# Attention over 2304 positions: one query tile's upper and lower value sums formed by one 129-column matmul, the lower one added afterwards on VectorE

## The reference, cut to what matters

```
xn   = groupnorm(x)
q, k, v = Wq xn, Wk xn, Wv xn              # per head: 64 channels x 2304 positions
attn = softmax over keys m of (q_n . k_m)  # no scaling by the root of 64
out  = sum over m of attn[n, m] v_m
y    = x + gamma * out + Wsc xn
```

## Time and profile before

| | |
|---|---|
| median of three runs | 3135.88 us |
| profiled execution, its own time | 3136.14 us |
| its span in the profile | 3134.4 us |
| PE busy | 3085.4 us (98%) |
| weight loads (PEld) | 2183.6 us (70%) |
| POOL busy | 2789.6 us (89%) |
| DVE busy, ACT busy | 2271.4 us (72%), 2244.6 us (72%) |
| mean granted TensorE clock | 0.997 |

### The profile page before, as it was taken

How to read it: one execution, slowest core, us unless ns; L and a number is a source line. 1 busy time by engine, 2 the same in 40 slices (tenths; PEclk the granted TensorE clock), 3 DMA queues, 4 the chain that set the end, 5 groups by cost and what they waited for, 6 DMA issues and landing times.

```text
span 3134.4 us, 119616 instructions
## 1 busy us (share of the span) xinstructions
PE 3085.4 (98%) x52307; PEld 2183.6 (70%) x52307; DVE 2271.4 (72%) x3623; ACT 2244.6 (72%) x4020; POOL 2789.6 (89%) x2040
## 2 busy tenths in 40 slices
PE   6999999999999999999999999999999999999998
PEld 4676777767767677776766767777776777777766
DVE  7677777777777777777777777777777777777774
ACT  5666787777676677777767677778776767667675
POOL 1788999999888899999888889999988989889899
PEclk9999999999999999999999999999999999999999
DMA  3111111110111111120112111111101010101011
GB/s 130 30 41 37 32 45 24 45 34 23 36 40 50 29 36 43 25 54 25 24 30 52 47 26 43 35 34 45 24 23 26 20 29 20 29 20 29 20 29 30
DMA packets 168968, 110.78 MB, mean 35 GB/s; under 512 B 120320, under 2 KB 166400, under 8 KB 168448
## 3 DMA queue, kind: packets, MB, share of 16 engines
q1 hardware_dynamic: 168448, 103.13, 12.5%
HBM read 56.10 MB, written 18.87 MB: 24 GB/s over the span
## 4 chain that ended last, share of the span: by engine, by line
PE 88%; POOL 5%; DVE 2%; ACT 1%; issue 1%; POOLq 0%; ACTq 0%; DVEq 0%
PE SL L440 24%; PE PJ L379 19%; PE MX L412 11%; PE OB L461 10%; PE OB L458 9%; PE OB L460 9%; PE PJ L376 6%; POOL PLO L940 5%; PE SL L435 1%; DVE mx L740 0%; DVE stat L896 0%; DVE xr L731 0%; DVE DF L690 0%; ACT QK L540 0%; DVE mx L743 0%
## 5 line engine op out<-in xcount | busy, mean ns | idle before, releaser
L940 POOL TENSOR_TENSOR PLO<-PE 128x768 f16<-128x768 f32 x1728 | 2550.6, 1499 | 278.4 <-ACT PE L554 267.0
L554 ACT ACTIVATE PE<-SL 128x768 f32<-128x768 f32 x1728 | 1307.4, 810 | 26.8 <-PE SL L440 26.6
L458 PE MATMUL OB<-V,PE 128*128 128x65 f16 x10368 | 1049.2, 193 | 7.2 <-POOL PLO L940 6.1
L460 PE MATMUL OB<-V,PE 128*128 128x64 f16 x10368 | 1049.3, 193 | 0.0
L461 PE MATMUL OB<-V,PLO 128*128 128x65 f16 x10368 | 1049.0, 196 | 0.0
L458 PEld LDWEIGHTS OB<-V,PE 128*128 128x128 bf16 x10368 | 965.4, 99 | 58.5 <-POOL PLO L940 12.2
L440 PE MATMUL SL<-QK 64*128 64x384 f16 x10368 | 1001.0, 323 | 0.1
L460 PEld LDWEIGHTS OB<-V,PE 128*128 128x128 bf16 x10368 | 962.9, 97 | 42.9
L562 ACT ACTIVATE MXC<-MX 128x384 f32<-128x384 f32 x864 | 423.5, 490 | 760.5 <-PE MX L412 760.5
L461 PEld LDWEIGHTS OB<-V,PLO 128*128 128x128 f16 x10368 | 963.8, 98 | 0.0
L743 DVE TENSOR_REDUCE mx<-MX 128x2 f32<-128x768 f32 x864 | 828.7, 959 | 82.7 <-PE MX L412 38.4
(11 more groups left out here) (104 smaller groups left out, 1238.1 us busy)
## 6 DMA issues: line engine op xcount, KB each, us to landing
gx<-x SPq DMA_DIRECT2D x36, 768.0 KB, 4.7
xr<-x SPq DMA_DIRECT2D x96, 192.0 KB, 2.4
out<-xr SPq DMA_DIRECT2D x96, 192.0 KB, 1.9
X<-x SPq DMA_DIRECT2D x6, 768.0 KB, 8.6
CR<-c SPq DMA_TRANSPOSE x96, 2.3
back<-half SPq DMA_TRANSPOSE x95, 2.8
QK<-wk SPq DMA_DIRECT2D x1, 1024.0 KB, 12.7
QK<-wv SPq DMA_DIRECT2D x1, 1024.0 KB, 13.4
```

The costliest lines, as they stand in the source:

```text
L458: pe.matmul(acc, upper, v[:, D:V1], start=k == 0 and h == 0 and i == 0, stop=False, skip_group_check=True)
L460: pe.matmul(acc[:, 0:D], upper, v[:, 0:D], start=False, stop=False, skip_group_check=True)
L554: act.activation(PE32[:, s % PB, :].rearrange("p (h n) -> p h n", h=2), SL[s % 2][:, :, 0:CH], ACT.Exp, scale=1.0 / SS).then_inc(s_exp, 1)
L940: nc.gpsimd.tensor_tensor(PLO[:, s % PB, :], PE32[:, s % PB, :], PE32[:, s % PB, :].bitcast(BF16)[:, 1:4 * CH:2], ALU.subtract).then_inc(s ...
```

## The change

In each step, the first query tile of the first head (h = 0, i = 0) no longer gets L458 and L460 but one matmul over all 129 columns of V, lower values, upper values and ones. It needs a stationary load less. The sum with the lower values now has 64 columns of its own in OB (0 to 63), and the six tiles of 66 columns start at column D = 64. After `evacuate` VectorE adds these 64 columns to the tile's part of Oe (`add_lower`, placed between `top_other` and the second `top` of m = 1, and ahead of `invert` at the end). A new semaphore `s_ol` tells that it is done; the first `weigh` of a chunk and the divisions wait for it.

```
-                    pe.wait_ge(s_oe, n)
+                    pe.wait_ge(s_ol, n)
...
-            acc = OB[:, (h * QT + i) * OW:(h * QT + i) * OW + AW]
+            acc = OB[:, D + (h * QT + i) * OW:D + (h * QT + i) * OW + AW]
...
-            pe.matmul(acc, upper, v[:, D:V1], start=k == 0 and h == 0 and i == 0, stop=False, ...)
-            pe.matmul(acc[:, 0:D], upper, v[:, 0:D], start=False, stop=False, ...)
+            if h == 0 and i == 0:
+                pe.matmul(OB[:, 0:V1], upper, v, start=k == 0, stop=False, ...)
+            else:
+                pe.matmul(acc, upper, v[:, D:V1], start=False, stop=False, ...)
+                pe.matmul(acc[:, 0:D], upper, v[:, 0:D], start=False, stop=False, ...)
...
     evacuate (ACT):
-        act.activation(Oe[:, :, :, :], OB[:, 0:2 * QT * OW] ...
+        act.activation(Oe[:, :, :, :], OB[:, D:D + 2 * QT * OW] ...
     divide (ACT, h == 0) and divide (DVE, last chunk):
+        wait_ge(s_ol, n + 1)
...
+    def add_lower(n):
+        dve.wait_ge(s_oe, n + 1)
+        nc.vector.tensor_tensor(Oe[:, 0, 0, 0:D], OB[:, 0:D], Oe[:, 0, 0, 0:D], ALU.add).then_inc(s_ol, 1)
...
     VectorE's loop, after top_other(U) and before top(U + 1):
+        if m == 1 and n:
+            add_lower(n - 1)
     VectorE's end:
+    add_lower(CHUNKS - 1)
     invert(CHUNKS - 1)
```

More of the change, by code:

```diff
@@ L212, in build @@
         s_oe = sem("s_oe")
+        s_ol = sem("s_ol")
         s_rc = sem("s_rc")
@@ L454, in weigh @@
                         p0 = h * CH + i * P
-                        acc = OB[:, (h * QT + i) * OW:(h * QT + i) * OW + AW]
+                        acc = OB[:, D + (h * QT + i) * OW:D + (h * QT + i) * OW + AW]
                         upper = PE32[:, s % PB, p0:p0 + P].bitcast(BF16)[:, 1:2 * P:2]
                         v = V[:, g % 2, k, h * V1:(h + 1) * V1]
-                        pe.matmul(acc, upper, v[:, D:V1], start=k == 0 and h == 0 and i == 0, stop=False,
-                                  skip_group_check=True)
-                        pe.matmul(acc[:, 0:D], upper, v[:, 0:D], start=False, stop=False, skip_group_check=True)
+                        if h == 0 and i == 0:
+                            pe.matmul(OB[:, 0:V1], upper, v, start=k == 0, stop=False, skip_group_check=True)
+                        else:
+                            pe.matmul(acc, upper, v[:, D:V1], start=False, stop=False, skip_group_check=True)
+                            pe.matmul(acc[:, 0:D], upper, v[:, 0:D], start=False, stop=False,
+                                      skip_group_check=True)
                         last = pe.matmul(acc, PLO[:, s % PB, p0:p0 + P], v[:, D:V1], start=False,
@@ L567, in evacuate @@
                     act.wait_ge(s_wt, n)
-                act.activation(Oe[:, :, :, :], OB[:, 0:2 * QT * OW].rearrange(
+                act.activation(Oe[:, :, :, :], OB[:, D:D + 2 * QT * OW].rearrange(
                     "p (h i x) -> p h i x", h=2, x=OW)[:, :, :, 0:AW], ACT.Copy).then_inc(s_oe, 1)
@@ L574, in divide @@
                     act.wait_ge(s_rc, n + 1)
+                    act.wait_ge(s_ol, n + 1)
                     act.wait_ge(s_al, n)
@@ L794, in divide @@
                 dve.wait_ge(s_rc, n + 1)
+                dve.wait_ge(s_ol, n + 1)
                 dve.wait_ge(s_al, n)
```

## The result

Over 20 runs of each the changed kernel took 3130.62 us against 3135.89 us; the ratio is 0.9983, with a 95% interval of 0.9977 to 0.9989. That is 5.27 us less, a gain that is clear of its interval and smaller than the 0.2% that the prediction had set as its mark. The profiled execution took 3130.39 us with a span of 3128.6 us.

What follows compares the result with a forecast made beforehand. TensorE (PE) was taken to bound the kernel until POOL's splits take over in chunk 90. 3136.14 - 5.7 (merged matmul) + 0.2 (tail) = 3130.6 us, or 3130.4 by the runs' median; 8 in 10 range 3122.5 to 3136.

Steps and rivals of the forecast that it cites:

- The bound and the 1618 steps: PE bounds until POOL's splits take over in chunk 90; only the 1618 `weigh` steps before that can gain.
- The merged matmul: First tile of each `weigh` step: one fixed matmul cost saved, 3.5 ns per step, 5.7 us; bounds 3.2 and 12.3 us.
- The signs: Expected in the trace: first tile about 88 ns instead of 92, other tiles unchanged, POOL taking the chain about 6 us earlier.
- The weight loads don't show in any of them.: PE's matmuls of three widths cost their columns plus a fixed 3 to 3.7 ns; loads of some 100 ns stay hidden.
- The addition: VectorE after `evacuate`: 0.24 us (0.18 to 0.56), ready 0.2 us before PE wants it, costing PE nothing.
- the wait binds: Rival, chance 0.09 with other costs: PE waits for `s_ol` at first `weigh` of 89 chunks, 18 us lost, 3148 us.
- VectorE idle for some 0.9 us: Sign on VectorE before L740: the addition's 0.24 us delay comes out of an idle time of 1.08 us.
- The tail: After the last matmul: addition ahead of the reciprocal adds 0.24 us (0.18 to 0.56); merging saves nothing at the lower clock.
- Only inside the tile: Rival, chance 0.18: in `weigh` only gaps inside the tile shrink, 2.0 ns per step, 3.2 us less, 3132.9 us.
- rate of short matmuls: Rival, chance 0.24: short matmuls' rate limits `weigh`; merging gains 5 to 7.6 ns per step, 8 to 12.3 us less.
- No cheaper: Rival, chance 0.06: the 129-column matmul costs as much as the two it replaces; only the tail counts, 3136.1 us.

Runs made afterwards that it cites:

- e9: Kernel before with a different form of `weigh` in each of a block's six chunks, one having a 16-column second matmul; 3123.61 us (before 3135.51).
- e1: Changed kernel without VectorE's addition and its semaphore, matmuls as changed; 3130.67 us, ratio 0.9986 to the kernel before.
- e2: Kernel before plus the 64-column addition into a spare tile with `s_ol` and PE's wait, matmuls as before; 3136.14 us, ratio 1.0002.
- e10: Changed kernel with a further 384-column addition ahead of the real one, so `s_ol` comes later, traced; 3136.03 us in one execution.
- e4: Changed kernel with all six tiles of a step given the 129-column matmul; 3112.0 us, ratio 0.9931 to the kernel before.
- e11: Changed kernel with the sums ordered so both operands change as rarely as they can; 3123.14 us, ratio 0.9959 to the kernel before.
- e12: The changed kernel as it is, run again on the chip of the rarest-change order; 3130.81 us, ratio 0.9984 to the kernel before.

## Why the prediction was right, step by step

- **The bound and the 1618 steps.** Right. The gain stops at POOL's takeover in chunk 90, and POOL's stage kept its length: 166.9 us against 166.8.
- **The merged matmul.** 3.5 ns per step were taken, between 2.0 and 7.6; 3.27 were measured. The bookkeeping was right (one matmul less, the same columns), the one fixed cost at all widths was not. The 56.7 ns read from the L376 rows are a mean in which the first of 18 starts is followed by 66.3 ns; the others are 55.8 ns apart, 2.5 ns over the columns (over 171 such groups). L458 and L460, where they aren't late, take 29.2 ns, about 2 ns over theirs, and the late starts make up the rest of the 3.7. At 2.5 ns the gain would have been the 4.0 us that the prediction also gives. So 3.5 ns is an average of unlike things, chosen between bounds, and that it came within 0.3 ns is in part luck. The closer look, by the gaps inside a tile, would have misled: by it the gain was 2.0 ns, with the late start taken for a cost of changing tile. (The 32.7 ns of the hand-over come from rounded starts; in the same 36 matmuls it is 34.4, and 29.0 inside a tile.) In the changed kernel the merged matmul of a block's second step takes 59.2 ns, more than the 57.2 reckoned with, but the late start behind its L465 is gone (29.2 ns to the next tile in place of 34).
- **The signs.** "About 88 ns" for the first tile and "the other tiles unchanged" hold only in the second step of a block (88.4 ns). In the first step the first tile takes 85.8 ns and three tiles behind it change. The lateness moves from place to place, and only the block's whole length can be priced. What makes a start late stays open.
- **"The weight loads don't show in any of them."** Columns and a fixed cost fail at the narrow end. e9 shows a floor near 28 ns for a pair of load and matmul, and the load may be what sets it. It did no harm, because the 64 columns of the removed pair take 26.7 ns by themselves; for a cut to 16 columns the same reckoning would have promised 20 ns and got 6.
- **The addition.** 0.24 us were reckoned, 0.215 measured, hidden as said: 0.05 us at most in e1 and e2. Its rival (the wait binds) stayed where it was put, at 0.09. Its price was too high. By the prediction's rule, e10's `s_ol` comes 0.14 us too late (1022.02, with the last matmul of the projection at 1021.88), and with 0.1 us for the restart that makes 0.24 us per chunk. Paid were 0.04 and 0.01. The sign "VectorE idle for some 0.9 us" failed as well: it is 1.07 us, since the addition fits in without delaying L748.
- **The tail.** +0.24 reckoned. From the start of the last copy to that of the division it was 0.76 us before (3128.95 to 3129.71) and is 0.89 (3123.08 to 3123.97): 0.13, as reciprocal and addition overlap. At the lower clock the pitch is 0.05 us for 65 columns, as in the earlier trace rows.

```profile
3123.08 0.50 ACT L572 ACTIVATE Oe<-OB 128x390 f32<-128x390 f32 x1 [4.89 <-PE OB L465]
...
3123.61 0.22 DVE L767 TENSOR_TENSOR Oe<-OB,Oe 128x64 f32<-128x64 f32 x1 [0.49 <-ACT Oe L572]
3123.75 0.18 DVE L773 RECIPROCAL rc<-Oe 128x6 f32<-128x6 f32 x1
3123.97 0.56 DVE L807 TENSOR_TENSOR attn<-Oe,rc 128x384 f32<-128x384 f32 x1
```

- **The rivals.** "Only inside the tile" (2.0 ns) and "rate of short matmuls" (5 to 7.6) both miss 3.27 ns as sums; e4, with 4.07 ns for each further matmul, lies between forecast and the latter. The mechanism of the latter, catching up on late starts, is not refuted: the first tile of a block did lose 7.5 ns, and the tile behind it gave 4.4 back. "No cheaper" is refuted by e1.

## What to carry to other kernels

Where matmuls overlap, read what one costs from the length of a whole block of starts; single gaps move when anything is changed, and a mean over a group hides a long first gap. Then look at the order before the count: here the same matmuls in another order were worth more (7.3 us) than one matmul less per step (5.3). A wait that is added on the bound engine costs only what it ends later than the work already handed to that engine, and two traces with one half of the change each show that to 0.05 us.

## What the runs showed of the hardware that was not expected

- From a pair of weight load and matmul to the next it is 28.1 ns on average with 16 columns and 29.2 with 65, late starts left out (e9).
- The pace of pairs of 64 and 65 columns depends on the order of the sums: 7.3 us over 1618 steps, 4.5 ns per step (e11 against e12).
- An instruction of VectorE with two inputs from SBUF lasted up to 5.8 us beside POOL at work without a pause, where its least was 0.62, and ended 0.41 us after POOL ran dry; PE stood idle for 4.5 us, and the granted clock was then 0.5 for some 7 us (e4).
- A load and its matmul can start together 0.06 us after the end of the instruction that released them, in all 89 chunks (e10: 57 to 59 ns for the matmul).
